# Two layers on a 4096-node graph: the second layer's adjacency loads go out on two queues, x is read back in pieces, and the closing hyperbolic formula takes one log and one tanh

## The reference

```python
h = jnp.maximum(_layernorm(x), 0.0)
x = x + _L0_gnn_ref(h, adj, adj, ptr, Wq, bq, Wk, bk, Wv, bv)   # attention inside graphs
h = jnp.maximum(_layernorm(x), 0.0)
x = x + _L1_gnn_ref(h, adj, W)                                  # hyperbolic mean
```

```python
XW  = mobius_matvec(W, h)
gamma = maximum(2 / (1 - sum(XW * XW)), 1e-15)
two_mean = (adj @ (gamma * XW)) / clamp_abs(adj @ (gamma - 1))
a_mean = two_mean / (1 + sqrt(maximum(1 - sum(two_mean ** 2), EPS)))
n   = norm(a_mean);  alpha = sum(adj, axis=-1)
AXW = tanh(alpha * artanh(n)) * a_mean / n          # artanh and tanh of a number per row
v   = relu(artanh(norm(AXW)) * AXW / norm(AXW))     # logmap0, then relu
out = tanh(norm(v)) * v / norm(v)                   # expmap0
```

## Time and profile before

| | |
|---|---|
| Time, median of 3 runs | 860.93 us (858.45 to 861.71) |
| Profiled execution: its own time | 860.4 us |
| Profiled execution: span | 858.6 us |
| PE busy in the span | 754.5 us (88%) |
| DVE busy | 664.4 us (77%) |
| ACT busy | 491.3 us (57%) |
| Moved by DMA | 157.13 MB, 183 GB/s on average |

### The profile page before, as it was taken

One profiled execution on the slowest core, in us unless ns is written; L12 is line 12 of the kernel. 1 busy time (PEld: TensorE's weight loads), 2 busy tenths in 40 slices (PEclk: granted clock), 3 DMA queues, 4 the chain that ended last, 5 costly groups with the idle time before them and its releaser, 6 DMA issues.

```text
span 858.6 us, 15125 instructions
## 1 busy us (share of the span) xinstructions
PE 754.5 (88%) x4989; PEld 693.8 (81%) x4996; DVE 664.4 (77%) x1370; ACT 491.3 (57%) x897; POOL 47.7 (6%) x96
## 2 busy tenths in 40 slices
PE   5999789999999999994665889999999999999780
PEld 4888677787778888783565889999999999999780
DVE  6778668878877888775585568888888888888865
ACT  2444366677776777676562335555555555555774
POOL 0000011000101000000000000000000000000340
PEclk9999989999999999998786999999999999999995
DMA  5115376776677776635409989999899889989631
GB/s 136 50 57 214 134 283 228 287 286 230 229 259 255 279 287 235 227 103 120 95 1 219 245 182 199 184 185 186 179 183 184 180 179 180 181 178 186 134 113 49
DMA packets 53373, 157.13 MB, mean 183 GB/s; under 512 B 9040, under 2 KB 30800, under 8 KB 47184
## 3 DMA queue, kind: packets, MB, share of 16 engines
q1 hardware_dynamic: 53328, 156.60, 68.8%
HBM read 148.16 MB, written 8.42 MB: 182 GB/s over the span
## 4 chain that ended last, share of the span: by engine, by line
PE 62%; DVE 15%; DMA 7%; SPq 4%; issue 4%; ACT 4%; DVEq 3%; ACTq 0%
PE bank L591 47%; PE bank L702 8%; DMA adjL<-in_adj 3%; DVE least L1420 3%; DMA adjU<-in_adj 2%; DVE adjT_lo L1360 2%; SPq L419 2%; PE bank L688 2%; PE bank L657 2%; DVE least L1404 2%; SPq L483 1%; DVE X_lo L1338 1%; DVE bank L1352 1%; DVE v L1221 1%; PE bank L583 1%
## 5 line engine op out<-in xcount | busy, mean ns | idle before, releaser
L591 PE MATMUL bank<-X_hi,adjT_hi 128*128 128x258 f32 x1024 | 296.1, 289 | 36.6 <-DVE adjT_lo L1360 36.6
L591 PE MATMUL bank<-X_hi,adjT_lo 128*128 128x258 f32 x1024 | 294.1, 287 | 0.0
L591 PE MATMUL bank<-X_lo,adjT_hi 128*128 128x258 f32 x1024 | 294.0, 287 | 0.0
L591 PEld LDWEIGHTS bank<-X_hi,adjT_hi 128*128 128x128 f32 x1024 | 198.9, 194 | 39.4 <-DVE adjT_lo L1360 26.2
L591 PEld LDWEIGHTS bank<-X_lo,adjT_hi 128*128 128x128 f32 x1024 | 199.4, 195 | 0.0
L591 PEld LDWEIGHTS bank<-X_hi,adjT_lo 128*128 128x128 f32 x1024 | 199.0, 194 | 0.0
L909 ACT CAST adjT_hi<-bank 128x1024 fp32r<-128x1024 f32 x96 | 97.4, 1014 | 131.5 <-PE bank L591 88.5
L1352 DVE STREAM_TRANSPOSE bank<-adjL 128x1024 f32<-128x1024 f32 x96 | 119.6, 1246 | 36.2 <-DMA adjL<-in_adj 36.1
L1360 DVE TENSOR_TENSOR adjT_lo<-bank,adjT_hi 128x1024 fp32r<-128x1024 f32 x96 | 116.1, 1210 | 16.7 <-ACT adjT_hi L909 16.4
L702 PE MATMUL bank<-values,probT 128*128 128x256 f32 x512 | 121.2, 381 | 4.9 <-ACT probT L945 4.8
L702 PEld LDWEIGHTS bank<-values,probT 128*128 128x128 f32 x512 | 93.2, 190 | 18.7 <-ACT probT L945 7.2
(11 more groups left out here) (168 smaller groups left out, 1119.8 us busy)
## 6 DMA issues: line engine op xcount, KB each, us to landing
adjL<-in_adj SPq DMA_DIRECT2D x128, 512.0 KB, 9.1
adjU<-in_adj SPq DMA_DIRECT2D x32, 1024.0 KB, 5.7
adjL<-in_adj SPq DMA_DIRECT2D x16, 2048.0 KB, 10.0
x_scratch<-x SPq DMA_DIRECT2D x16, 258.0 KB, 3.5
xin<-in_x SPq DMA_DIRECT2D x8, 512.0 KB, 3.8
xt<-in_x SPq DMA_DIRECT2D x16, 256.0 KB, 3.3
x_all<-x_scratch SPq DMA_DIRECT2D x4, 1024.0 KB, 17.6
out_x<-res SPq DMA_DIRECT2D x8, 512.0 KB, 2.9
```

Of the source, the lines that this page charges most:

```text
L591: last = pe.matmul(dst, a[i][a_cols], b[j][b_cols], start=(k_first and n == 0), stop=(k_last and n == 2))
```

## The change

Four things are changed.

- **Two queues.** From tile 2 on SP issues quadrants 0 and 1 of a tile, and ACT quadrants 2 and 3 (`mean_adj_far`), after its `adj_high` of the last chunk of tile t - 2. ACT's halves are counted by semaphores of their own (`d_adj_far`), and DVE waits for both. Tiles 0 and 1 are still loaded by SP alone, with the quadrants in the order 0, 2, 1, 3.
- **x in pieces.** x is read back by 16 DMAs of 256 KB (two row tiles each) instead of 4 of 1 MB: two at the start and one in each round of the loop over pairs of tiles.
- **Tiles 2 and 3 sooner.** SP asks for both before it waits for `s_x1_out` and `s_lo`; that wait now stands ahead of x alone.
- **A shorter finish.** artanh(tanh(z)) is taken as min(z, FURTHEST). The parts `finish_product`, the second `finish_series` and `finish_log` go, and with them one log and one tanh on ACT. Three instructions and their drains are added to `finish_scaled`.

```diff
-FINISH_FUNCTIONS = [(ACT.Sqrt, "squares", "roots"), (ACT.Ln, 5, 5), (ACT.Tanh, 2, 2), (ACT.Ln, 5, 5),
-                    (ACT.Tanh, 1, 3)]
-FINISH_CHUNKS = (1, 2, 4, 5, 7)
+FINISH_FUNCTIONS = [(ACT.Sqrt, "squares", "roots"), (ACT.Ln, 5, 5), (ACT.Tanh, 1, 3)]
+FINISH_CHUNKS = (1, 2, 4)
...
-            def mean_adj(t, par):
-                for a in range(QD):
+            def mean_adj(t, par, quarters_of_it=(0, 1)):
+                for a in quarters_of_it:
                     sp.dma_start(adjL_q[a * RB:(a + 1) * RB, par], adj_q[t, a]).then_inc(d_adj[par], 16)
...
-                mean_adj(0, 0)
+                mean_adj(0, 0, (0, 2, 1, 3))
...
+            def x1_back(i):
+                sp.dma_start(x1_all_2[:, i], x1_pairs[i]).then_inc(s_x1_all, 16)
+
+            for t in range(2):
+                mean_adj_next(t, t)
             sp.wait_ge(s_x1_out, 16 * HT)
             sp.wait_ge(s_lo, T)
             for t in range(2):
-                mean_adj_next(t, t)
-                for part in range(2 * t, 2 * t + 2):
-                    sp.dma_start(x1_all[:, part * HT // 2:(part + 1) * HT // 2, :],
-                                 x1_dram[part * N // 4:(part + 1) * N // 4, 0:D].rearrange("(t p) d -> p t d", p=P))\
-                      .then_inc(s_x1_all, 16)
+                x1_back(t)
+
             with sp.Fori(1, HT - 1) as i:
                 for par in range(2):
                     mean_adj_next(2 * i + par, par)
+                x1_back(i + 1)
...
+            def mean_adj_far(t, par):
+
+                act.wait_ge(d_turned, place_of(t - 2, NQ - 1) + 1)
+                for a in (2, 3):
+                    act.dma_start(adjL_q[a * RB:(a + 1) * RB, par], adj_q[t, a]).then_inc(d_adj_far[par], 16)
...
                     adj_high(NQ * t + q, q)
+                    if q == NQ - 1 and not (isinstance(t, int) and t >= T - 2):
+                        mean_adj_far(t + 2, par)
...
                 if q == 0:
-                    dve.wait_ge(d_adj[par], arrived)
+                    dve.wait_ge(d_adj[par], later + 16 * QD)
+                    wait(dve, d_adj_far[par], later)
...
             def finish_scaled(c):
 
                 artanh_end(V[2][:, c], V[5][:, c], V[6][:, c], V[7][:, c])
...
+                tt(V[2][:, c], V[2][:, c], alpha[:, c], ALU.mult)
+                dve.drain()
+                dve.scalar_tensor_tensor(out=V[0][:, c], in0=V[2][:, c], scalar=FURTHEST, in1=V[0][:, c], op0=ALU.min,
+                                         op1=ALU.mult)
                 dve.drain()
                 tt(V[1][:, c], V[0][:, c], roots[:, 2, c], ALU.mult)
                 dve.drain()
...
-            FINISH_PARTS = (finish_root, finish_mean, finish_series, finish_scaled, finish_product, finish_series,
-                            finish_log, finish_exp)
+            FINISH_PARTS = (finish_root, finish_mean, finish_series, finish_scaled, finish_exp)
```

More of the change, by code:

```diff
@@ L1 @@
+import math
 import concourse.bass as bass
@@ L18 @@
 CLIP = 1.0 - 1e-7
+FURTHEST = math.atanh(1.0 - 2.0 ** -23)
 TINY_ARG = 0.25
@@ L216, in graph_layers_kernel @@
         x1_all = place("x1_all", [P, T, D], "qx")
+        x1_all_2 = x1_all[:, :, :].rearrange("p (i j) d -> p i j d", j=2)
         qx_v = qx[:, :, :].rearrange("p (g j) c -> p g j c", j=BPC)
@@ L310, in graph_layers_kernel @@
         d_adj = [sem("mean_adj_in0"), sem("mean_adj_in1")]
+        d_adj_far = [sem("mean_adj_far_half_in0"), sem("mean_adj_far_half_in1")]
         d_turned = sem("adj_chunk_turned")
@@ L452, in _ @@
                 sp.wait_ge(s_expL, HT)
-                mean_adj(1, 1)
+                mean_adj(1, 1, (0, 2, 1, 3))
                 x1_store(step_at(HT - 1))
@@ L549, in _ @@
                 steps(pool, pair)
-            pool.wait_ge(s_x1_all, 16 * 4)
+            pool.wait_ge(s_x1_all, 16 * HT)
             for t in range(FIRST_BATCH):
@@ L1048, in _ @@
             adj_high(6)
+            mean_adj_far(2, 0)
             adj_high(7)
+            mean_adj_far(3, 1)
             def mean_tile(t, par):
@@ L1347, in adj_turn @@
             def adj_turn(t, par, q, n):
-                arrived = 16 * QD * (t // 2 + 1) if isinstance(t, int) else 8 * QD * t - 8 * QD * par + 16 * QD
+                later = 8 * QD * (t // 2) if isinstance(t, int) else 4 * QD * t - 4 * QD * par
                 if q == 0:
-                    dve.wait_ge(d_adj[par], arrived)
+                    dve.wait_ge(d_adj[par], later + 16 * QD)
+                    wait(dve, d_adj_far[par], later)
                 dve.transpose(turned[n_slot(n, q)].rearrange("p (b s r) -> p s b r", s=QD, r=RB),
@@ L1559, in finish_scaled @@
                 artanh_end(V[2][:, c], V[5][:, c], V[6][:, c], V[7][:, c])
-                tt(V[2][:, c], V[2][:, c], alpha[:, c], ALU.mult).then_inc(s_f, 1)
-            def finish_product(c):
-                function_done()
-                tt(V[0][:, c], V[0][:, c], V[2][:, c], ALU.mult)
+                tt(V[2][:, c], V[2][:, c], alpha[:, c], ALU.mult)
                 dve.drain()
-                tt(V[1][:, c], V[0][:, c], roots[:, 1, c], ALU.mult)
-                dve.drain()
-                ts(V[2][:, c], V[1][:, c], EPS, CLIP, ALU.max, ALU.min)
-                ts(V[1][:, c], V[1][:, c], EPS, None, ALU.max)
-                dve.drain()
-                artanh_start(V[2][:, c], V[5][:, c], V[6][:, c])
-            def finish_log(c):
-                artanh_end(V[2][:, c], V[5][:, c], V[6][:, c], V[7][:, c])
-                tt(V[0][:, c], V[0][:, c], V[2][:, c], ALU.mult)
+                dve.scalar_tensor_tensor(out=V[0][:, c], in0=V[2][:, c], scalar=FURTHEST, in1=V[0][:, c], op0=ALU.min,
+                                         op1=ALU.mult)
                 dve.drain()
@@ L1640, in _ @@
             mean_scales(T - 1, 1, T)
-            dve.wait_ge(s_x1_all, 16 * 4)
+            dve.wait_ge(s_x1_all, 16 * HT)
             dve.wait_ge(d_sq, 2)
```

1 line of the change is left out of this document (added).

## The result

The changed kernel took **849.19 us** (median of 4 runs, 848.49 to 850.18) beside 861.04 us for the kernel before (4 runs, 858.45 to 861.71): a ratio of 0.9869, 95% interval 0.9846 to 0.9892. It is faster, by 11.9 us, half of the 23.6 forecast, and it lies outside the predicted range (829.6 to 847).

What follows compares the result with a forecast made beforehand. PE was taken to bound most of the kernel (62% of the last chain). Terms 3.5 + 11.5 + 4.8 + 3.8 = 23.6 us off 860.4 gave 836.8; the median adds 0.5, so 837 us, range 829.6 to 847.

Steps and rivals of the forecast that it cites:

- The long part: Mean-stage loop after the start, where PE sets the pace: extra DMA issues and x's pieces stay hidden, priced at nothing.
- the engines never run dry: Loop loads: ACT asks about 3 us after the turn, within the 5.1 us the first half flows; no cost.
- 2.6 us are free: Loop, each two tiles: 23.2 us against 20.6 of loads leave 2.6 free; a piece of x takes 0.75.
- POOL's later x holds up only the stores: Loop and end: later x delays only stores of the first 24 tiles, outlasted by DVE's last additions; no cost.
- The start: Start of the mean stage: tile 2 lands 3.5 us sooner, and later waits and slow starts save 11.5 us.
- tile 2: Start: asked for sooner and by two queues, it lands 3.5 us sooner, between 1.4 and 5.7.
- The later waits and slow starts: Start, tiles 3 and 4: PE's waits of 3.94 and 3.92 us and two slow clock starts go, 11.5 us.
- The finish: Shorter finish: 4.8 us behind the last product (bounds 4.3 and 5.0), 3.8 us in the first batch (0 to 4.45).
- two queues do no better than one: Rival for tile 2's load: both queues share 204 GB/s, 1.4 us gained instead of 3.5; 839 us, chance 0.24.
- wait of 3.9 us: Rival at the start: a tile still comes late, one wait and its 2.0 us slow start stay; 843 us, chance 0.09.
- The clogged loop: Rival between tile loads: interleaved x pieces take 5.1 us, not 0.75, costing 35 us; 872 us, chance 0.06.
- The point from which a piece costs: Loop, within the clogging rival: a piece of x begins to cost time at 2.6 us.

Runs made afterwards that it cites:

- versions 7: The changed kernel with x's pieces one round sooner (three at the start), still issued by SP ahead of the far half; 844.4 us.
- version 6: The changed kernel with x's pieces issued by ACT behind the odd tile's far half, and one round sooner; 832.81 us.
- version 11: The changed kernel with x as before, in four 1 MB transfers at the start behind tile 3's near half, none in the loop; 849.36 us.
- 2: The changed kernel with one queue: SP issues all four quadrants of every tile, x's piece behind the odd tile; 843.5 us.
- version 8: The changed kernel with all four quadrants issued by SP and x's pieces one round sooner; 837.22 us.
- versions 1: The changed kernel with the loop's piece of x issued by ACT behind the odd tile's far half, not by SP ahead of it; 842.19 us.
- version 9: As version 6, but SP brings quadrants 0 and 2 and ACT 1 and 3, so each queue writes both partition halves; 837.26 us.

## Why the prediction was right or wrong

**The long part, "priced at nothing", is the step that failed.** It measured +11.3 us (in DVE's turns; versions 7 and 6, which differ in the place of x's piece, are 844.4 - 832.8 = 11.6 us apart). Two of its reasons fell:

- "The second half's 1 MB is due 5.1 us after the first starts to flow ... so the engines never run dry." They did not run dry (and ACT asked 1.4 us after SP for an odd tile and 0.02 for an even one, not 3). But that was the wrong question: an odd tile is complete when its *last* request is served, and x's piece, asked for 0.4 us ahead of the far half, was served ahead of it.
- "2.6 us are free, and a piece at 348 GB/s takes 0.75." This is an account of throughput over a round of two tiles, and it holds (in after 0.10 of the DMA engines were busy from 617 to 621). The limit was the way of one tile: asking, latency, near half, x, far half, four turns, asking again. In the kernel before it was worth 621.89 - 609.4 = 12.5 us, 9.6 for the turns where PE does not hold them up and 0.2 to the next asking, 22.3; PE's round is 23.0. Its slack was 0.7 us, and x's piece makes it 1.4 longer (14.1 against 12.7 in version 11). The row that I read as "PE does not notice", a wait of 0.40 us for a load, was the sign that this loop was nearly closed.

**"POOL's later x holds up only the stores" failed as well**, and cost the end 3.6 us (versions 7 and the change; 7.5 and 8.1 in the pairs 2 and 8, 1 and 6, where PE sets the pace up to the end). The stores were late and covered, as I said. But POOL's additions, pressed together into one stretch, run beside DVE's lows and slow them.

**The start was right, tile 2 under-sized.** I took 3.5 us between bounds of 1.4 and 5.7; it was 4.9. SP asked when I had it to (the whole mean stage lies 1.7 us earlier in this profile), but ACT at the same moment and not 1.3 us later, as its request went out while its rounding still ran, and from then on the two queues moved 270 to 315 GB/s. Of the 4.9, 2.7 come from SP asking sooner (version 8 with one queue: 43.6 against 46.3) and the rest from the second queue. The later waits and slow starts gave 10.7 against 11.5, and 11.7 in version 6. The granted clock is 0.50 from 461 to 465 us, 0.97 to 471 and 1.00 from there on, as said.

**The finish was right in both terms:** 9.0 against 8.6 by itself. In the changed kernel the 4.8 behind the last product show (1.76 us in place of 6.54). The bounds given for them, 4.3 and 5.0, are not what a tenth of 0.95 us of steps makes (0.1 either way).

**The rivals.** That two queues do no better than one was wrong for tile 2 and the even tiles (asked together), and right for the odd ones (asked apart). No wait of 3.9 us stayed at the start. The clogged loop was the right place, and the wrong mechanism: x's packets did not mix with those of adj and slow down, the piece was served nearly by itself, near 164 GB/s, and made the tile 1.4 us later, not 5.1. The point from which a piece costs, 2.6 us, came from the throughput account; the loop of one tile puts it at 0.7. The other terms of the sum were sound: with the loop and the end mended, version 6, which is not the kernel that was predicted, gives 860.9 - 832.8 = 28.1 us where the change was to give 23.6.

What stays open: why two requests 1.0 to 1.45 us apart are served one after the other and two that are 0.02 to 0.12 us apart side by side. The last two tiles lie between. Tile 31, whose halves are asked for 0.9 us apart in versions 1, 6 and 11, lands one quadrant after the other and is complete 12.5 or 12.6 us after the first asking; tile 30, at 0.14 or 0.15 us, is complete after 10.6 or 10.7, and after 13.0 in version 9, where the quadrants under way share a half. Where between 0.15 and 0.9 us the one turns into the other, and why, no run shows.

## What to carry to other kernels

A load that is asked for again only when its buffer has been used up is a loop of latencies; compare the *whole way* of one buffer (asking, everything queued ahead of its last byte, its use) with the pace, and not the bytes of a round with the bandwidth. A small transfer that shares the queue order with such a load is best asked for behind its last piece; between its pieces it cost 1.4 us a round here. Work that is only put off is not free: look at what it will then run beside.

## What the runs showed of the hardware

- Two queues that are asked at the same moment, each for its own half of the partitions, moved 254 to 324 GB/s in the windows above; where the two quadrants under way lay in the same half, 199 to 217, like one queue alone. The Trainium skill ("SBUF — State Buffer", section "Can I just issue two DMAs to hit both halves?") puts the gain of two such DMAs at 6% and says that they serialize. Here, into opposite halves, they moved up to half as much again where they were asked together, and where they were asked 0.9 us or more apart they serialized; the measurement decides. What the same page says of which partitions share ports (section "Door 1: The DMA port swizzle", with the two halves of 64 on different ports) agrees with version 9.
- A low with both inputs in SBUF took 2.85 to 6.00 us beside POOL's additions where these ran without a pause, and at most 1.43 beside short bursts of them; one with an input in PSUM took 1.18 to 1.23 beside either. The same page (section "Who interferes with whom") says that a VectorE instruction with two SBUF inputs contends with a GpSimd instruction that reads SBUF; the rows agree.
- ACT's DMA request went out 0.18 us after the start of the rounding ahead of it in its list, while that still ran (1.01 us). A semaphore that the rounding raises at its end is therefore no way to ask at the same time.
